# Group-norm statistics of image 0 moved beside the weight preparation, and less zeroing ahead of layer 0

## What is computed

```python
def _gn(v, G=32, eps=1e-5):
    ...
    m = jnp.mean(g, axis=(2, 3, 4), keepdims=True)
    s = jnp.var(g, axis=(2, 3, 4), keepdims=True)
    return ((g - m) / jnp.sqrt(s + eps)).reshape(v.shape)

# layer 0: 1x1 conv to 384 channels, depthwise 3x3, q*k in the frequency
# domain of 8x8 patches, layer norm over channels, times v, 1x1 conv to 64
x = x + _L0_conv_ref(_gn(x), ...)
# layer 1: involution 3x3 with kernels made from batch-normed features,
# softplus, 3x3 conv, softplus
x = x + _L1_conv_ref(_gn(x), ...)
```

## Time and profile before

| | us |
|---|---|
| median of 3 runs | 9162.08 |
| lowest, highest | 9158.47, 9182.94 |
| the profiled execution | 9166.47 |
| its span, first to last instruction | 9164.7 |
| PE busy | 8542.7 (93%) |
| DVE busy | 7484.3 (82%) |
| ACT busy | 6350.6 (69%) |
| POOL busy | 4819.6 (53%) |

### The profile page before, as it was taken

How to read it: one execution, slowest core, us unless ns; L and a number is a source line. 1 busy time by engine, 2 the same in 40 slices (tenths; PEclk the granted TensorE clock), 3 DMA queues, 4 the chain that set the end, 5 groups by cost and what they waited for, 6 DMA issues and landing times. The chain is left out here.

```text
span 9164.7 us, 170682 instructions
## 1 busy us (share of the span) xinstructions
PE 8542.7 (93%) x57838; PEld 4864.3 (53%) x57838; DVE 7484.3 (82%) x9864; ACT 6350.6 (69%) x8676; POOL 4819.6 (53%) x2752
## 2 busy tenths in 40 slices
PE   0999999999999999999999999999887999999999
PEld 0666666666666666666666666666432333333333
DVE  4788788788888878878887777778767999999999
ACT  0777777677777767777776777777406888888888
POOL 1444434344344344444443444434207999999999
PEclk9999999999999999999999999999998999999999
DMA  6122222222222222222212122122394555555555
GB/s 141 47 61 65 50 61 63 54 61 50 65 61 50 65 54 58 65 50 61 65 46 53 43 50 51 45 48 51 85 234 96 120 119 118 119 118 121 119 120 117
DMA packets 618296, 715.70 MB, mean 78 GB/s; under 512 B 44382, under 2 KB 577348, under 8 KB 594352
## 3 DMA queue, kind: packets, MB, share of 16 engines
q1 hardware_dynamic: 618160, 713.88, 33.4%
HBM read 549.03 MB, written 164.70 MB: 78 GB/s over the span
## 5 line engine op out<-in xcount | busy, mean ns | idle before, releaser
L633 PE MATMUL banks<-w_hi,hi_lo 128*128 128x256 f16 x18432 | 2407.1, 277 | 87.0 <-DVE hi_lo L935 87.0
L633 PEld LDWEIGHTS banks<-w_hi,hi_lo 128*128 128x128 f16 x18432 | 1760.3, 100 | 926.2 <-issue 523.7
L591 POOL TENSOR_TENSOR u_im<-q_im,k_swap 128x512 f32<-128x512 f32 x512 | 652.0, 1273 | 1834.4 <-ACT q_im L829 1747.5
L1442 POOL TENSOR_TENSOR part_sum<-part_sum,prod 128x1024 f32<-128x1024 f32 x660 | 1561.3, 2366 | 53.1
L967 DVE SCALAR_TENSOR_TENSOR v_s<-banks,tap_w,v_s 128x512 f32<-128x512 f32 x2048 | 1534.7, 749 | 54.6 <-ACT v_s L818 0.3
L1471 PE MATMUL banks<-z,conv_w 128*128 128x512 f32 x3128 | 1575.7, 619 | 0.0
L803 ACT ACTIVATE qk<-banks,inv_wscale 128x512 f32<-128x512 f32 x1024 | 706.4, 690 | 1221.2 <-PE banks L633 1215.7
L594 POOL TENSOR_TENSOR u<-u,u_im 128x512 f32<-128x512 f32 x512 | 726.4, 1419 | 1069.6 <-DVE u L944 1069.6
L633 PE MATMUL banks<-w_lo_pair,hi_pair 128*128 128x256 f16 x6144 | 1017.7, 275 | 0.0
L600 POOL TENSOR_TENSOR u<-u,u_mean 128x512 f32<-128x512 f32 x512 | 533.0, 1041 | 797.5 <-DVE u_mean L975 797.5
L944 DVE TENSOR_TENSOR u<-q_re,banks 128x512 f32<-128x512 f32 x512 | 349.6, 683 | 636.0 <-ACT q_re L831 635.7
(11 more groups left out here) (252 smaller groups left out, 15735.4 us busy)
## 6 DMA issues: line engine op xcount, KB each, us to landing
xr<-in_x_dram SPq DMA_DIRECT2D x258, 640.0 KB, 9.2
xb<-y_scratch SPq DMA_DIRECT2D x268, 320.0 KB, 4.7
xa<-y_scratch SPq DMA_DIRECT2D x268, 256.0 KB, 5.3
x_res<-in_x_dram SPq DMA_DIRECT2D x258, 256.0 KB, 4.0
out_dram<-res SPq DMA_DIRECT2D x258, 256.0 KB, 3.3
y_scratch<-ys SPq DMA_DIRECT2D x256, 256.0 KB, 3.9
yc<-y_scratch SPq DMA_DIRECT2D x256, 256.0 KB, 5.5
xs<-in_x_dram SPq DMA_DIRECT2D x92, 512.0 KB, 7.2
```

The source lines that it names most:

```text
L591: nc.gpsimd.tensor_tensor(u_im[:], q_im[:], k_swap[:], ALU.mult).then_inc(u_made, 1)
L633: r = pe.matmul(out, px, w, start=n == 0, stop=n == 13)
L1442: nc.gpsimd.tensor_tensor(part_sum[:], prod[0][:] if n == 0 else part_sum[:], prod[n + 1][:], ALU.add)\
```

## The change

It does three things. First, block 2 is merged into block 1. The chunks are loaded from ACT's queue instead of SP's, into four buffers instead of two, and DVE's `bn_stats` of chunks 0 and 1 stand ahead of its wait for the weights, those of chunks 2 and 3 between the two halves of the weight work, and those of chunks 4 to 8 with the final steps behind it. Second, the zero rows of `y1` are no longer written from `zrow` in block 1. In layer 0, behind the loads of the first two strips, SP copies them from the 9 rows of zeros that stand at the end of x in DRAM, in 7 DMAs from DRAM to DRAM; it waits for them at the end of the block. Third, POOL's nine memsets are gone; DVE zeroes the edge rows and columns alone, in 16 memsets, and signals `buffers_zeroed`.

```diff
+            NXC = 4
+            xc = tsb("xc", [P, NXC, CH * W])
...
-                sp.wait_ge(zeroed, 1)
-                sp.dma_start(y1[:, 0:R, :], zrow[:, 0:R, :]).then_inc(stored, 16)
-                n = 16
-                for r0 in range(R + ROWS, Y1R, 18):
-                    k = min(18, Y1R - r0)
-                    sp.dma_start(y1[:, r0:r0 + k, :], zrow[:, 0:k, :]).then_inc(stored, 16)
-                    n += 16
-                sp.wait_ge(stored, n)
...
+            @blk.scalar
+            def _(act):
+                for i in range(NC):
+                    if i >= NXC:
+                        act.wait_ge(chunk_used, i - NXC + 1)
+                    for h in range(2):
+                        row = 1 + 2 * CH * i + CH * h
+                        act.dma_start(xc[C * h:C * h + C, i % NXC, :].rearrange("p (r w) -> p r w", w=W),
+                                      A["x"][:, row:row + CH, :]).then_inc(chunk_loaded[i % NXC], 16)
+                group_norm_root(act, asked, answered, tmp)
...
+                def chunks(i0, i1):
+
+                    for i in range(i0, min(i1, NC)):
+                        v.wait_ge(chunk_loaded[i % NXC], 32 * (i // NXC + 1))
+                        for n in range(NST):
+                            last = v.bn_stats(x_stats[:, 2 * i + n // 4, 6 * (n % 4):6 * (n % 4) + 6],
+                                              xc[:, i % NXC, 512 * n:512 * n + 512])
+                        last.then_inc(chunk_used, 1)
...
+                chunks(0, 2)
                 v.wait_ge(loaded, 16 * len(loads))
                 v.wait_ge(v_loaded, 16 * 11)
                 v.wait_ge(transforms_loaded, 16 * 28)
...
                 v.tensor_tensor(wmax[:, 4:5], wmax[:, 0:1], wmax[:, 3:4], ALU.max).then_inc(maxed, 1)
+                chunks(2, 4)
                 v.wait_ge(maxed, 2)
...
+                chunks(4, NC)
+                v.wait_ge(chunk_used, NC)
...
                 for b in range(2):
                     load(R * b, b)
                     load_res(R * b + 1, b)
+
+                n = 0
+                for r0, r1 in ((0, R), (R + ROWS, Y1R)):
+                    for row in range(r0, r1, XTRA):
+                        rows = min(XTRA, r1 - row)
+                        sp.dma_start(y1[:, row:row + rows, :], A["x"][:, 1 + ROWS:1 + ROWS + rows, :]).then_inc(edges_stored, 16)
+                        n += 16
                 run(sp, body)
+                sp.wait_ge(edges_stored, n)
...
-                nc.gpsimd.memset(eps[:], LN_EPS)
-                for t in xr + [xn, hi_all, hl_all] + hi_ind + hi_side:
-                    last = nc.gpsimd.memset(t[:], 0.0)
-                last.then_inc(buffers_zeroed, 1)
...
+                v.memset(eps[:], LN_EPS)
+                for b in range(2):
+                    v.memset(xr[b][0:C, 0, :], 0.0)
+                    v.memset(xr[b][C:P, SL - 1, :], 0.0)
+                    v.memset(hi_side[b][C:P, W:WP, :], 0.0)
+                    for col in (0, WP - 1):
+                        v.memset(hi_ind[b][C:P, col, :], 0.0)
+                for t in (hi_all, hl_all):
+                    for col in (0, WP - 1):
+                        v.memset(t[:, col, :], 0.0)
+                v.memset(xn[:, :, SL:SLP], 0.0).then_inc(buffers_zeroed, 1)
```

More of the change, by code:

```diff
@@ L94, in build_program, with group_norm_params, then, group_norm_root @@
         x_stats = sb("x_stats", [P, NB, 24])
+        def group_norm_params(blk_sems, v, layer, mv, tmp, i0, i1, averages):
+            step, asked, answered, count = blk_sems
+            images = slice(i0, i1)
+            def then(ins):
+                count[0] += 1
+                ins.then_inc(step, 1)
+                v.wait_ge(step, count[0])
+            mean, var = mv[:, :, 0], mv[:, :, 1]
+            then(v.tensor_tensor(tmp[:, 0, :], mean, mean, ALU.mult))
+            then(v.tensor_tensor(tmp[:, 1, :], tmp[:, 0, :], var, ALU.add))
+            then(v.tensor_copy(tmp[:, 0, :], mean))
+            v.tensor_copy(tmp[:, 2, :], mean).then_inc(asked, 1)
+            v.wait_ge(answered, 1)
+            then(v.tensor_copy(tmp[:, 0:2, :], averages[:, 0:2 * (i1 - i0)].rearrange("p (a i) -> p a i", a=2)))
+            then(v.tensor_tensor(tmp[:, 2, :], tmp[:, 0, :], tmp[:, 0, :], ALU.mult))
+            then(v.tensor_tensor(tmp[:, 2, :], tmp[:, 1, :], tmp[:, 2, :], ALU.subtract))
+            v.tensor_scalar(tmp[:, 2, :], tmp[:, 2, :], 0.0, GN_EPS, ALU.max, ALU.add).then_inc(asked, 1)
+            v.wait_ge(answered, 2)
+            then(v.reciprocal(gn_scale[:, layer, images], tmp[:, 2, :]))
+            then(v.scalar_tensor_tensor(gn_bias[:, layer, images], tmp[:, 0, :], -1.0, gn_scale[:, layer, images],
+                                        ALU.mult, ALU.mult))
+            return then
+        def group_norm_root(act, asked, answered, tmp):
+            act.wait_ge(asked, 2)
+            act.activation(tmp[:, 2, :], tmp[:, 2, :], ACT.Sqrt).then_inc(answered, 1)
+        IT = NB // NI
+        LEAD = 2 if NI > 1 else 0
         with ExitStack() as ph:
@@ L109, in build_program @@
             b_sel = tsb("b_sel", [P, 2])
-            zrow = tsb("zrow", [C, 18, W])
             wmax = tsb("wmax", [P, 10])
@@ L122, in build_program @@
             maxed = ph.enter_context(nc.semaphore("weight_max"))
-            zeroed = ph.enter_context(nc.semaphore("zeros_made"))
-            stored = ph.enter_context(nc.semaphore("zeros_stored"))
+            CH = 2 * R
+            NC = (IT + LEAD) // 2
+            NST = CH * W // 512
+            NXC = 4
+            xc = tsb("xc", [P, NXC, CH * W])
+            mv = tsb("mv", [P, 1, 2])
+            tmp = tsb("tmp", [P, 3, 1])
+            chunk_loaded = [ph.enter_context(nc.semaphore(f"chunk_loaded{i}")) for i in range(NXC)]
+            chunk_used = ph.enter_context(nc.semaphore("chunk_used"))
+            gn_step = ph.enter_context(nc.semaphore("gn0_step"))
+            asked = ph.enter_context(nc.semaphore("gn0_asked"))
+            answered = ph.enter_context(nc.semaphore("gn0_answered"))
             turned = ph.enter_context(nc.semaphore("v_rows_turned"))
@@ L189, in _ @@
                 last.then_inc(v_cleared, 1)
-                nc.gpsimd.memset(zrow[:], 0.0).then_inc(zeroed, 1)
                 pool.wait_ge(maxed, 1)
                 nc.gpsimd.partition_all_reduce(wmax[:, 6:8], wmax[:, 4:6], P, RMAX).then_inc(maxed, 1)
+            @blk.scalar
[8 more added lines that the diff above has]
+                group_norm_root(act, asked, answered, tmp)
+            @blk.tensor
+            def _(pe):
+                pe.wait_ge(asked, 1)
+                for q in range(4):
+                    for a in range(2):
+                        made = pe.matmul(bank[0][32 * q:32 * q + 32, a:a + 1], pair_avg[:, 32 * q:32 * q + 32], tmp[:, a, :],
+                                         start=True, stop=True)
+                made.then_inc(answered, 1)
             @blk.vector
@@ L278, in _ @@
                 then(v.tensor_copy(w_lo_one[C:P, 1, :], btap[C:P]))
[L280 to L354, removed]
-                for col, src in ((0, gn_scale), (1, gn_bias)):
[L356 to L369, removed]
@@ new lines, in _ @@
+                chunks(4, NC)
+                v.wait_ge(chunk_used, NC)
+                v.bn_aggr(mv[:, 0, :], x_stats[:, 0:IT, :].rearrange("p a k -> p (a k)")).then_inc(gn_step, 1)
+                v.wait_ge(gn_step, 1)
+                then_gn = group_norm_params((gn_step, asked, answered, [1]), v, 0, mv, tmp, 0, 1, bank[0])
+                for col, src in ((0, gn_scale), (1, gn_bias)):
+                    then_gn(v.tensor_copy(tab0[:, 0:S, col:col + 1], src[:, 0:1, 0:1].to_broadcast([P, S, 1])))
@@ L420, in build_program @@
             ind_loaded = tsem("ind_loaded")
+            edges_stored = tsem("edges_stored")
             buffers_zeroed = tsem("buffers_zeroed")
```

## The result

| | before | after |
|---|---|---|
| median of 10 runs, us | 9164.55 | 9137.71 |
| lowest, highest | 9158.47, 9182.94 | 9131.87, 9149.69 |
| profiled execution, its span | 9166.47, 9164.7 | 9131.87, 9130.1 |
| first matmul of layer 0 at | 224.56 | 196.56 |
| from there to the end | 8940.1 | 8933.5 |

The ratio of the times is 0.9969, with a 95% interval of 0.9960 to 0.9977: 28 us less, 21 to 37 by the interval. Forecast was 9141, 20.8 less than the median of the first three runs. The two profiled spans differ by 34.6 us, of which 28.0 lie ahead of layer 0's first matmul. The other 6.6 lie behind it. There the program is the same. Across the profiled executions of this study that stretch took from 8933 to 8960 us, and the one profiled here, the lowest of all, is the fastest of the changed kernel's ten; so the 6.6 us are put down to scatter between executions.

A forecast was written before the change was run, and what follows sets the result against it. PE was taken as busy nearly throughout, so only time before its first layer 0 matmul, at 224.56 us, could be gained: 3.4 (merged block) + 17.4 (memsets) = 20.8; 9162.1 - 20.8 = 9141 us, range 9084 to 9151.

The forecast's parts named there:

- the memsets: Before layer 0's first strip load: POOL's 19.76 us, wholly on the path, give way to DVE's 2.4; gain 17.4 us.
- the merged block: Weight and chunk work ahead of layer 0: layer 0's block begins at 171.4 instead of 174.84 us; gain 3.4 us.
- rivals 1 and 2: Weights get several packets per chunk packet, time 9118, chance 0.18; or queues share by bytes, time 9088, chance 0.27.
- t: Time at which all weights have landed, 33.33 us before the change; at 96 the merging would gain nothing.
- t + 78.6: Start of layer 0's block: DVE's fixed work after the weights land takes 78.6 us, with no chunk load late.
- t = 92.8: Landing of the weights beside the chunk loads: 68 us for `v_rows`, then 24.8 us for the rest as before.
- the 68: Landing of `v_rows`, first in SP's queue: six chunks' turns last 65 us, then 2.8 us for its remaining 40 packets.
- the 0.07 us for a small packet: Time of one `v_rows` packet on a DMA engine, from 88 packets per engine and about 7.7 us to landing.
- 48 turns: Six chunks of 8 packets per engine, pending without a gap; one weight packet moves in each turn.
- the one-for-one value: Upper bound for the weights' landing: engines take one packet from each queue in turn, 1.23 us per chunk packet.
- The copies: Zero-row copies ahead of strip 2's load in layer 0: cost 0 under 71.5 us of cover, then one-for-one.
- Rival 3: Layer 0's DRAM-to-DRAM copies run at 35 GB/s, strip 2 lands 65 us late; 44 us slower, 9206, chance 0.03.

The follow-up runs named there:

- four times the copies: The changed kernel with 18 more DRAM-to-DRAM copies of 9 zero rows behind its seven; single run, first matmul of layer 0 at 196.3 us.
- 1 KB: The changed kernel with each chunk DMA cut into two that take every other row, so packets are 1 KB; ratio to before 0.9945.
- 4 KB: The changed kernel with each chunk DMA cut into two taking alternate groups of 4 rows, so packets are 4 KB; ratio to before 0.9977.
- two buffers: The changed kernel with two chunk buffers instead of four; single run, first matmul of layer 0 at 194.7 us.

## Why the prediction was right, and where its steps were off

The forecast was that the memsets give 17.4 us and the merged block little, since the chunk loads would push the weights from 33 to some 93 us. The mechanism is what the trace shows from about 8 us on, and rivals 1 and 2 (the weights get several packets for one, or share by bytes) are refuted by the equal counts of packets. The size of the merged block's gain was off: 10.3 us where 3.4 were forecast, since it is the small difference of t to 96, and t came 6.2 us earlier. Step by step:

- *The memsets:* 17.4 forecast, 17.54 in the profile after (19.76 to 2.22), 17.7 when done alone.
- *From the weights to the block,* t + 78.6: measured 77.95, and the statement that no chunk is late held.
- *t = 92.8:* measured 86.6. This is the mis-sized term, and accounts for 6.2 of the 7.2 us by which the first matmul came earlier than forecast. The prediction had `v_rows` landed at 68 and 24.8 us for the rest; in the trace it landed at 62.66 and the rest took 24.0. What made the 68 too large is the 0.07 us for a small packet. It was worked out from the 7.7 us to landing, which are not the time of the packets: in the trace of before SP's queue moved 1325 packets from 2 to 3 us, 83 for each engine, which is 0.012 us for one. The two products with 0.07, 48 and 40 packets or 3.4 and 2.8 us, are then 1.1 us together, and the sum gives 62.6 for `v_rows` and 87.4 for t.
- *The turns behind it:* two more parts were off. The queue of `v_rows` was not served in turn from the first packet: between 5 and 10 us SP's queue moved 747 packets, 47 of the 88 for each engine, beside 80 of ACT's, and fell into step from about 8 us on. And six chunks are more than 48 turns: ACT's queue moves 161 packets in 10 us, of which 32 are small like those counted in rows 6, so 10 for a chunk and engine. With 47 ahead and 60 turns the 88 packets of `v_rows` had gone by about 51 us, 11 us before it landed; what held the landing is not shown, and that it fell with the end of the chunks, as the sum has it, is partly luck. What the first burst hastened was, as it seems, SP's release. I had put the hold at the issues of `wh`, with the queue in the state of 8.5 us; it was at `bh`, and SP was free at 57.0, some 94 packets for each engine in, with 28.1 us of issuing left.
- *Between the bounds:* I took the one-for-one value because the engines were full with packets one after another. That was the reading that decided the forecast, and it was not certain: it had 0.46. The Trainium skill (DMA: Bandwidth & Descriptors, Queues, rings and completion order) has the round-robin at packet granularity, and all three sizes of packets agree with it: 162 and 162, 513 and 516, 1647 and 1643. A packet that holds several descriptors, as it says is typical, did not show: the turns went by single packets as the trace counts them (14 and 14, 22 and 22 in a microsecond). The bursts of SP's queue, 501 beside 17 from 6 to 7 us, are an exception that neither explains.
- *The copies:* cost 0, as forecast. The cover of 71.5 us was right, the price behind it too high: 5.6 us for 9.2 of waiting in the one run that has it.
- *Rival 3* (slow copies from DRAM to DRAM) fell: with four times the copies the stretches moved 279 to 327 GB/s and not 35.
- *The chances:* the measured gain of 0.31% lies at the bound of what can be told from no change, nearer to "faster" than the forecast's 0.23%; the range, 9084 to 9151, was wide since it had to hold a t of 33.

The measured time is 3.3 us below the forecast. That agreement is closer than the steps were, and is partly luck: the first matmul was forecast 7.2 us too late, and the gain was taken off a median of three runs that lies 2.5 us below that of ten. The gain itself, 26.8 us by the medians with an interval of 21 to 37, was forecast as 20.8, just outside it.

## What to carry to other kernels

In this kernel a transfer that filled the DMA engines with large packets, put on a second queue, did not share with small loads by bytes: the small ones moved one packet for each large one, and a preload whose bytes would take 13 us (2.74 MB at 210 GB/s, an estimate) was pushed from 33 to 87 us. Where the same shows in a trace, hold the bulk back until the many-packet loads have landed; here starting it 33 us later made the kernel's first part 30 us shorter. Cutting its packets to the size of the small ones, 1 KB, gave 25 us, cutting them to 4 KB only 2. Look for the price at the issuing engine: here it stood in a single DMA issue that lasted 53 us, with everything behind it in that engine's program.

## What the runs showed of the hardware

- Two queues with work pending moved the same number of packets, within 1% from 20 to 30 us with chunk packets of 16, 4 and 1 KB. In the first 12 us there are stretches in which they did not: 726 packets of SP's queue beside 59 of ACT's from 5 to 8 us with 16 KB, 510 beside 86 from 9 to 11 us with 4 KB.
- SP's issues ran ahead of the data only to a point: held at `bh` with `v_rows`, `wh` and `w_dw` (88 + 8 + 72 packets for each engine) ahead of it. Where the limit lies exactly was not measured. The hold ended when SP's queue had moved 94 packets for each engine (after), 89 (1 KB), 85 (4 KB), 101 (two buffers) and 93 (four times the copies), near the 88 of `v_rows` each time, at 57.0, 10.3, 10.2, 22.6 and 56.8 us.
- Reading x ran at 214 GB/s from one queue with packets of 16 KB (before, 75 to 150 us), at 220 with 1 KB (60 to 75 us), and at 226 from two queues. The stretches of 10 us with copies from DRAM to DRAM between the loads ran at 279 to 327.
- A pause of PE was followed by a lower clock. With four times the copies PE waited 3.4 us, and the windows (us, then busy time and count of each engine, granted clock, DMA share, GB/s) read

```profile
246.00:256.00 10.00, 6.62 (x36) 2.94 (x32) 1.49 (x3) 8.71 (x11) 2.53 (x2) 0.91 0.14 56
256.00:266.00 10.00, 10.00 (x80) 7.01 (x80) 9.85 (x17) 8.79 (x12) 3.41 (x3) 0.75 0.01 2
266.00:276.00 10.00, 10.00 (x87) 6.65 (x87) 7.21 (x12) 8.59 (x12) 5.52 (x5) 1.00 0.01 2
```

  where the changed kernel has a clock of 1.00 in the same three. Nine of the 128x256 matmuls took 2.10 us right behind the pause and 1.16 ahead of it, near the ratio of the two levels, 1.2 and 2.4 GHz. So part of the 5.6 us is the clock, not the wait.
